# Search and placing of a mixture-of-experts router moved into the shared feed-forward loop

## The chip, the core and the metric

The kernel runs on one core of a Trainium2 chip. Its engines run side by side, each with its own instruction stream: TensorE (PE in the profile; its weight loads are PEld) multiplies matrices, VectorE (DVE) and ScalarE (ACT) work elementwise, GpSimd (POOL) does elementwise work and issues DMAs whose rows are picked by a list of indices, SyncE (SP) issues DMAs. They wait for each other on semaphores only. The metric is device time in microseconds (us), the median of several runs.

## The reference, cut to what matters

64 images of 224 x 224 are cut into 196 patches each, so N = 12544 tokens of width 192. Behind the attention (here only the input of this part) each token passes a shared feed-forward network and, if it is chosen, some of eight experts:

```python
probs = jax.nn.softmax(flat @ Wr, axis=-1)             # flat: [12544, 192], 8 experts
topk_p, topk_i = jax.lax.top_k(probs, 2)
topk_p = topk_p / jnp.clip(topk_p.sum(-1, keepdims=True), 1e-09)
capacity = 3920                                        # ceil(n * 2 / 8 * 1.25)
score = jnp.where(assigned, w_tok, -jnp.inf)           # per expert and token
order = jnp.argsort(-score, axis=1)[:, :capacity]      # the 3920 best tokens of each expert
dispatch = flat[order]
gate = jax.nn.silu(jnp.einsum('ech,ehi->eci', dispatch, w1))
up = jnp.einsum('ech,ehi->eci', dispatch, w3)
expert_out = jnp.einsum('eci,eih->ech', gate * up, w2) * weight_sel[..., None]
routed = routed.at[order.reshape(-1)].add(expert_out.reshape(-1, h))
shared = jax.nn.silu(flat @ s1) * (flat @ s3) @ s2
out = routed + shared
```

## The kernel before, in words

The program has three blocks, one behind the other; a block ends when the last engine has come to its end. `attention` makes the tokens and writes their rows, their transposed columns and the router's logits to DRAM. Then comes `routing` (L868), then `ffn` (L1315).

**`routing`.** Instead of sorting, it searches for each expert's lowest score that still gets in, its level. All scores lie as `key` in 128 partitions by 8 experts by 98 tokens. First the choices: softmax, the best and the second best expert of each token, their shares, the keys (DVE, L1017 to L1042). SP writes the keys to DRAM and reads them back with 16 partitions per expert (`by_expert`, 784 elements each, L916 to L918), then loads the shared network's weights (L1150). ScalarE casts these to their upper fp16 halves (L1156), and GpSimd makes the lower halves in ten instructions (L940, L942). Meanwhile DVE runs 15 rounds of search, each settling two bits of the level by three trial values. A round: the trial values (L978), three passes that mark which scores reach a trial (`count_from`, L1009), 24 fp16 matmuls that add up the marks over partitions (L952), a reduction of what is left (L1058), a comparison with the capacity (L982), and three predicated copies into `level` (L1063). The steps wait for one another, and PE and DVE take turns. Then the level goes to DRAM and comes back broadcast to all partitions (SP, L921, L924), and the placing gives each kept token its slot: comparisons, two running sums (L1014) with one matmul each (L966), and sums over the experts for the first and the second choice.

**`ffn`, shared part.** 24 units of 512 tokens and one of 256 (`shared_units`, a loop over pairs of units for the middle 22). Per unit the hidden width of 768 is done in six chunks, two at a time: `tensor_pair` computes gate and up of a pair of chunks for the unit (PE, L1206 to L1214), and behind each pair `tensor_out` does a third of the output matmuls of the unit before (L1235 to L1237). ScalarE takes the silu of a chunk (L1251), DVE multiplies (L1270, `multiplied`), ScalarE casts the product to its upper half (L1245), DVE makes the lower half (L1263). The gate and up banks are double; the pair after next needs the multiplies of the pair before it. Once per unit DVE and ScalarE also split the next unit's tokens (L1188, L1191; L1179 to L1182), and DVE adds the finished outputs to the residual (L1623). SP loads tokens and residual rows (L1354, L1357).

**Dispatch.** Beside the shared part GpSimd writes the tokens' numbers and shares into a table in DRAM, by slot: 196 scatters of 128 rows (L1417), on two semaphores. Each waits until the one before the last has landed, so that two are in flight. SP first loads eight small pads into the id tiles (L1348), works through the shared units, then waits for the dispatch and loads the ids of the first four expert units (L1370).

**`ffn`, expert part.** 64 units of 490 rows. GpSimd gathers the rows by ids (L1429), ScalarE and DVE split them, SP transposes them by DMA (L1386), PE, ScalarE and DVE work as in the shared part, and GpSimd adds the results to the output by index (L1440).

Of the kernel before, what the change touches and what calls it, by code (L numbers as in the profile page):

```python
# [17 lines left out]
ALU = mybir.AluOpType  # L18
# [849 lines left out]
def routing(nc, dram, slot_of, entry, T):  # L868


    ROUNDS, TRIALS, CHUNKS = 15, 3, 128 // E
    CUT = N // CHUNKS // 8
    with ExitStack() as ctx:
# [3 lines left out]
        def sem(name):  # L877
            return ctx.enter_context(nc.semaphore(name))

        full3 = [128, E, PER]  # L880
        probs, first, second, keep, key, scratch, running, carry = (
            sb(n, full3) for n in ("probs", "first_choice", "second_choice", "keep", "key", "scratch", "running", "carry"))
        top, norm, best, w1, w2 = (sb(n, [128, PER]) for n in ("top", "norm", "best", "w1", "w2"))
        before = sb("before", [128, 128])
        same = sb("same", [128, 128])
        same16 = sb("same16", [128, 128], F16)
        rank = sb("rank", [128, E])
        base = sb("base", [128, E])
        place = sb("place", [128, E])
        bits = sb("bits", [128, ROUNDS * TRIALS], I32)  # L890
        by_expert = sb("by_expert", [128, 8 * CUT])
        reached = sb("reached", [128, TRIALS, 8 * CUT], F16)
        level = sb("level", [128, 2], I32)
        levels = sb("levels", [128, E, 2], I32)
        trial = sb("trial", [128, TRIALS], I32)
        enough = sb("enough", [128, TRIALS], I32)
        count = sb("count", [128, TRIALS])
        total = ctx.enter_context(nc.psum_tensor("total", [128, 512], F32))
        offset = ctx.enter_context(nc.psum_tensor("offset", [128, 2, 512], F32))
        (logits_in, bits_in, consts_in, entry_in, shifted, powered, vec, keyed, keys_out, keys_in, compared, totalled,  # L900
         settled, level_out, levels_in, enlarged, ranked, summed, spacer) = map(sem, (
             "logits_in", "bits_in", "route_consts_in", "entry_in", "shifted", "powered", "route_steps", "keyed", "keys_out",
             "keys_in", "compared", "totalled", "settled", "level_out", "levels_in", "enlarged", "ranked", "prefix_summed",
             "route_spacer"))
        block = ctx.enter_context(nc.Block())
        constants = ((rank, "rank"), (same, "same"), (before, "before"), (base, "base"))

        @block.sync
        def _(sp):
            sp.dma_start(probs[:], dram["logits"].rearrange("e (p t) -> p e t", p=128)).then_inc(logits_in, 16)  # L910
            for dst, src in constants:
                sp.dma_start(dst[:], dram[src]).then_inc(consts_in, 16)
            sp.dma_start(bits[:], dram["bits"]).then_inc(bits_in, 16)
            sp.dma_start(entry[:], dram["entry"]).then_inc(entry_in, 16)
            sp.wait_ge(keyed, 1)
            sp.dma_start(dram["keys"].rearrange("e (p t) -> p e t", p=128), key[:]).then_inc(keys_out, 16)  # L916
            sp.wait_ge(keys_out, 16)
            sp.dma_start(by_expert[:], dram["keys"].rearrange("e (c x) -> (e c) x", c=CHUNKS)).then_inc(keys_in, 16)  # L918
            load_weights(sp, dram, T, E)
            sp.wait_ge(settled, 1)  # L920
            sp.dma_start(dram["level"], level[:]).then_inc(level_out, 16)  # L921
            sp.wait_ge(level_out, 16)
            each = dram["level"].rearrange("(e c) x -> c e x", c=CHUNKS)[0:1]
            sp.dma_start(levels[:], each.to_broadcast([128, E, 2])).then_inc(levels_in, 16)  # L924
            sp.wait_ge(T.raw_in, 48)

        @block.scalar
        def _(act):
            act.wait_ge(shifted, 1)
            nc.scalar.activation(probs[:], probs[:], ACT.Exp).then_inc(powered, 1)  # L930
            act.wait_ge(T.raw_in, 48)
            weights_hi(nc, T, 0)

        @block.gpsimd
        def _(pool):
# [3 lines left out]
            for raw, hi, lo, last in lower_parts(T, 0):  # L939
                nc.gpsimd.tensor_scalar(raw, raw, WEIGHT_SCALE, None, ALU.mult).then_inc(enlarged, 1)  # L940
                pool.wait_ge(enlarged, n + 1)
                ins = nc.gpsimd.tensor_tensor(lo, raw, hi, ALU.subtract).then_inc(enlarged, 1)  # L942
                pool.wait_ge(enlarged, n + 2)
                n += 2
                if last:
                    pool.sem_inc(T.weights_lo, 1)

        @block.tensor
        def _(pe):
            def total_of(t):  # L950
                for c in range(8):
                    last = nc.tensor.matmul(total[:, t * CUT:(t + 1) * CUT], same16[:],  # L952
# [307 lines left out]
def vector_unit(nc, dve, T, g, slot, n, split, split_at):  # L1260
# [5 lines left out]
    for m in range(MI):  # L1266
# [8 lines left out]
        if m == split_at:  # L1275
            split()
# [485 lines left out]
```

## Time and profile before

| | us |
|---|---|
| three runs: median, lowest, highest | 3433.06, 3431.37, 3438.18 |
| the profiled execution, its own time | 3431.96 |
| its span in the trace | 3430.2 |
| attention | to about 1631 |
| choices, search, placing | to 1668.1, 1758.3, 1783.3 |
| first matmul of the shared part | 1795.65 |
| SP comes to the first ids | 2237.54 |
| expert part at full pace | from about 2264 |

The profile page gives busy shares of PE 91%, DVE 71%, ACT 45% and POOL 40% over the whole span. Over so many stages these say little, and the stages are read apart: a view of windows gives each engine's busy time between two points, TensorE's granted clock (1.00 is 2.4 GHz, 0.50 is 1.2 GHz) and the share of time in which the 16 DMA engines were busy. The timeline gives single instructions with their start and duration. A group line gives count, mean and idle time before, with who ended it.

### The profile page before, as it was taken

What the parts mean: (1) busy time and instruction counts of PE and PEld (TensorE: products, weight loads), DVE (VectorE), ACT (ScalarE), POOL (GpSimd) and SP (SyncE); (2) the same over time, 40 slices, a digit from 0 to 9 for tenths busy, and PEclk for the clock granted to TensorE, in tenths of its full rate; (3) what the DMA queues carried; (4) which work ended last, traced back from release to release, by engine and by line L of the source; (5) the groups of instructions that cost most, each with busy time, mean ns of one, the idle gap of its engine ahead of it and who ended that gap; (6) DMA issues with size and microseconds to landing.
All of it is one profiled execution on the core that took longest, in us unless ns stands there. A gap on an engine that the chain in (4) does not pass through costs nothing. (4 is left out here: it accounts for less than half of the span.)

```text
span 3430.2 us, 72008 instructions
## 1 busy us (share of the span) xinstructions
PE 3138.3 (91%) x26164; PEld 2153.2 (63%) x26164; DVE 2433.1 (71%) x4832; ACT 1557.6 (45%) x3287; POOL 1373.6 (40%) x1170
## 2 busy tenths in 40 slices
PE   6999999999999999998129999989999999999997
PEld 5777777777777777766125555556565566566664
DVE  6999999999999999997655555555545455455543
ACT  2445444544454454543004444444555455455543
POOL 1322233223322332222205555036665565556664
PEclk9899999999999999985559999999999999999999
DMA  3333233323332333322111222234554545445443
GB/s 105 74 74 80 69 86 84 75 64 86 88 74 67 81 87 74 75 44 54 44 52 48 77 67 72 74 91 76 98 95 71 99 76 97 92 73 101 75 73 42
DMA packets 461611, 260.21 MB, mean 76 GB/s; under 512 B 339103, under 2 KB 442879, under 8 KB 457183
## 3 DMA queue, kind: packets, MB, share of 16 engines
q1 hardware_dynamic: 393632, 196.42, 24.0%
q0 software_dynamic: 54400, 49.00, 10.0%
q10 hardware_dynamic: 13262, 10.66, 0.9%
q8 instruction: 188, 3.08, 0.4%
q14 instruction: 129, 1.06, 0.1%
HBM read 107.98 MB, written 68.15 MB: 51 GB/s over the span
## 5 line engine op out<-in xcount | busy, mean ns | idle before, releaser
L1270 DVE SCALAR_TENSOR_TENSOR ffn_hidden<-ffn_up,ffn_silu 128x490 f32<-128x490 f32 (+2 forms) x534 | 350.6, 670 | 690.2 <-ACT ffn_silu L1251 653.7
L689 POOL TENSOR_TENSOR weights<-weights,x_pair 128x400 f32<-128x400 f32 x384 | 395.3, 1029 | 830.6 <-DVE weights L561 819.6
L1251 ACT ACTIVATE ffn_silu<-ffn_gate 128x490 f32<-128x490 f32 (+2 forms) x534 | 301.5, 582 | 722.8 <-PE ffn_up L1214 722.4
L1440 POOL DMA_INDIRECT out_rows<-done,ids x256 | 408.2, 1594 | 401.2 <-ACT done L1542 339.7
L613 DVE RECIPROCAL recip<-x_product 128x200 f32<-128x200 f32 x384 | 534.8, 1393 | 0.0
L1235 PE MATMUL ffn_out<-ffn_w_hi,ffn_hidden_hi 128*128 128x192 f16 (+1 forms) x2124 | 525.3, 247 | 2.2 <-DVE ffn_hidden_lo L1263 1.8
L1237 PE MATMUL ffn_out<-ffn_w_hi,ffn_hidden_lo 128*128 128x192 f16 (+1 forms) x2124 | 522.5, 246 | 0.0
L1236 PE MATMUL ffn_out<-ffn_w_lo,ffn_hidden_hi 128*128 128x192 f16 (+1 forms) x2124 | 522.5, 246 | 0.0
L747 PE MATMUL bank<-w_tok,patches 128*128 128x192 f32 x1536 | 342.8, 383 | 39.2 <-DVE minus_half L525 24.1
L1263 DVE TENSOR_TENSOR ffn_hidden_lo<-ffn_hidden,ffn_hidden_hi 128x490 f16<-128x490 f32 (+2 forms) x534 | 356.5, 668 | 16.2
L1245 ACT CAST ffn_hidden_hi<-ffn_hidden 128x490 f16<-128x490 f32 (+2 forms) x534 | 320.7, 601 | 85.7 <-DVE ffn_hidden L1270 85.7
L1429 POOL DMA_INDIRECT tokens<-dram_x,ids x256 | 281.3, 1099 | 176.9 <-DMA ids<-dram_table 90.9
L747 PEld LDWEIGHTS bank<-w_tok,patches 128*128 128x128 f32 x1536 | 300.8, 224 | 55.7 <-issue 27.8
L856 PE MATMUL y_sum<-v_held,weights 128*64 128x68 f32 (+1 forms) x1536 | 267.3, 258 | 45.3 <-DVE weights L569 45.2
L1417 POOL DMA_INDIRECT dram_table<-entry,slot_of x196 | 200.7, 1024 | 252.7 <-issue 170.7
L1235 PEld LDWEIGHTS ffn_out<-ffn_w_hi,ffn_hidden_hi 128*128 128x128 f16 (+1 forms) x2124 | 218.8, 103 | 110.2 <-issue 100.3
L420 ACT ACTIVATE x_pair<-score 128x400 f32<-128x400 f32 x384 | 192.8, 502 | 205.7 <-DVE weights L561 200.3
L435 ACT ACTIVATE weights<-x_pair 128x400 f32<-128x400 f32 x384 | 205.0, 534 | 170.3 <-PE y_sum L862 165.4
L740 PE MATMUL bank<-w_qkv,normed_t 96*128 96x192 f32 (+1 forms) x1024 | 276.6, 419 | 0.7 <-ACT normed_t L411 0.7
L858 PE MATMUL y_sum<-v,weights 128*64 128x51 f32 (+2 forms) x1536 | 252.6, 248 | 0.0
L1206 PE MATMUL ffn_gate<-ffn_tokens,ffn_w_hi 128*128 128x490 f16 (+2 forms) x534 | 198.9, 372 | 43.3 <-DVE ffn_tokens L1191 19.7
L740 PEld LDWEIGHTS bank<-w_qkv,normed_t 96*128 96x128 f32 x1024 | 182.3, 194 | 69.1 <-issue 5.1
(176 smaller groups left out, 6934.4 us busy)
## 6 DMA issues: line engine op xcount, KB each, us to landing
patches<-in_patches SPq DMA_DIRECT2D x32, 1176.0 KB, 5.3
ffn_raw<-in_w SPq DMA_DIRECT2D x18, 768.0 KB
dram_x_t<-x_t SPq DMA_DIRECT2D x32, 392.0 KB, 3.7
x_t<-dram_x_t SPq DMA_DIRECT2D x24, 512.0 KB, 5.4
base<-dram_h SPq DMA_DIRECT2D x24, 384.0 KB, 4.2
out_rows<-sums ACTq DMA_DIRECT2D x24, 384.0 KB, 4.7
v_held<-v SPq DMA_DIRECT2D x64, 102.0 KB, 2.3
dram_h<-h SPq DMA_DIRECT2D x32, 192.0 KB
```

Source lines behind the costliest of these rows:

```text
L613: nc.vector.reciprocal(recip[:, n % 2], x_product[:, n % 2]).then_inc(inverted, 1)
L689: nc.gpsimd.tensor_tensor(weights[:, n % 4], weights[:, n % 4], x_pair[:, n % 4, ::-1], ALU.mult)\
L740: last = nc.tensor.matmul(out, wide(lhs, k, t), rhs[:, k, 0:width], start=(k == 0), stop=(k == 1))
L747: last = nc.tensor.matmul(out, wide(patches[slot], i, n), tok_w[:, i, :], start=(i == 0), stop=(i == KP - 1))
L1235: nc.tensor.matmul(out, hi, w_hi[:, m, :], start=(m == 0), stop=False)
L1236: nc.tensor.matmul(out, hi, w_lo[:, m, :], start=False, stop=False)
L1237: last = nc.tensor.matmul(out, lo, w_hi[:, m, :], start=False, stop=(m == MI - 1))
L1245: nc.scalar.copy(T.hidden_hi[slot][:, m, 0:n], T.hidden[:, m % 2, 0:n]).then_inc(T.hi_ready, 1)
L1251: nc.scalar.activation(T.silu[:, m % 2, 0:n], T.gate[m % 2][:, 0:n], ACT.Silu, scale=1.0 / (TOKEN_SCALE * WEIGHT_SCALE)).then_inc(T.silued, 1)
L1263: nc.vector.tensor_tensor(T.hidden_lo[slot][:, m, 0:n], T.hidden[:, m % 2, 0:n], T.hidden_hi[slot][:, m, 0:n], ALU.subtract).then_inc(T.lo ...
L1270: nc.vector.scalar_tensor_tensor(T.hidden[:, m % 2, 0:n], T.up[m % 2][:, 0:n], HIDDEN_SCALE / (TOKEN_SCALE * WEIGHT_SCALE), T.silu[:, m % ...
L1440: nc.gpsimd.indirect_dma_start(out=dram["out"][:, :], out_offset=bass.IndirectOffsetOnAxis(ap=ids[i][0:height, t, 0:1], axis=0), in_=done[ ...
```

## The change

`routing` is cut in two. `choices` is a block of its own and keeps what leads to the keys; in it SP asks for the shared weights right behind the four constants, ahead of the bits table, the entries and the trip of the keys over DRAM. The search and the placing become 24 steps in `search_and_place`, numbered by s = 3g + part. DVE does step s of them in unit g of the shared part behind its part-th pair of chunks, between the lower half of the pair's first chunk and that of its second. The matmul that adds up a step's counts is done by PE in `add_counts`, behind `tensor_pair` and ahead of `tensor_out`.

- The counting pass now also writes the sum of its marks along the 784 elements (`accum_out`). So one fp32 matmul of 128x128 by 3 columns stands for 24 fp16 ones of 98 columns, and the reduction is gone.
- Steps 0 to 15 are the search, 15 also the last count, 16 gives the settled level, 18 to 23 are the placing. PE's matmul for step s waits for the counts of step s - 1.
- The settled level travels to DRAM and back by GpSimd's queue, in the shared block. GpSimd starts the dispatch when the slots are placed, behind unit 7.
- The scatters use four semaphores, so that four are in flight.
- SP's eight pad loads move from ahead of the shared units to behind them.
- The loop over the shared units is written out.

```diff
+def add_counts(nc, pe, R, s):
+    if 1 <= s <= SEARCHED:
+        pe.wait_ge(R.compared, min(TRIALS * s, TRIALS * ROUNDS + 1))
+        nc.tensor.matmul(R.total[:, 0:TRIALS], R.same[:], R.count[:], start=True, stop=True).then_inc(R.totalled, 1)
+    if s in (PLACING + 1, PLACING + 3):
+        n = (s - PLACING) // 2
...
+        pe.wait_ge(R.ranked, n + 1)
+        nc.tensor.matmul(R.offset[:, n * E:n * E + E], R.before[:], R.running[:, :, PER - 1], start=True, stop=True)\
+          .then_inc(R.summed, 1)
...
+def search_and_place(nc, dve, R, slot_of, s):
...
+        nc.vector.tensor_scalar(R.reached[:, t], R.by_expert[:], at.bitcast(F32), None, op, ALU.add,
+                                accum_out=R.count[:, t:t + 1]).then_inc(R.compared, 1)
...
+    if 1 <= s <= ROUNDS:
+        dve.wait_ge(R.totalled, s)
+        ts(R.enough[:], R.total[:, 0:TRIALS], float(CAP), ALU.is_ge)
+        dve.sem_inc(R.spacer, 1)
+        for t in range(TRIALS):
+            step(nc.vector.copy_predicated(level[:, 0:1], R.enough[:, t:t + 1], R.trial[:, t:t + 1]))
+            if t < TRIALS - 1:
+                dve.sem_inc(R.spacer, 1)
+    if s < ROUNDS:
+        tt(R.trial[:], level[:, 0:1].to_broadcast([128, TRIALS]), R.bits[:, s * TRIALS:(s + 1) * TRIALS], ALU.bitwise_or)
+        for t in range(TRIALS):
+            count_from(t, ALU.is_ge, R.trial[:, t:t + 1])
...
@@ vector_unit
+        if m % 2 and behind_pair is not None:
+            behind_pair(m // 2)
@@ shared_units
-    unit(0, 0, 0, WHOLE)
-    with eng.Fori(0, (SHARED - 3) // 2) as j:
-        unit(2 * j + 1, j, 1, WHOLE)
-        unit(2 * j + 2, j + 1, 0, WHOLE)
-    unit(SHARED - 2, (SHARED - 3) // 2, 1, WHOLE)
+    for g in range(SHARED - 1):
+        unit(g, g // 2, g % 2, WHOLE)
@@ ffn, gpsimd
+            pool.wait_ge(R.settled, 1)
+            pool.dma_start(dram["level"], R.level[:]).then_inc(R.level_out, 16)
+            pool.wait_ge(R.level_out, 16)
+            each = dram["level"].rearrange("(e c) x -> c e x", c=CHUNKS)[0:1]
+            pool.dma_start(R.levels[:], each.to_broadcast([128, E, 2])).then_inc(R.levels_in, 16)
+            pool.wait_ge(R.placed, 2)
+            pool.sem_inc(spacer, 1)
+            for n in range(2 * PER):
+                if n >= 4:
...
+                    pool.wait_ge(dispatched[n % 4], 16 * (n // 4))
+                    pool.sem_inc(spacer, 1)
+                nc.gpsimd.indirect_dma_start(
```

## Rows read from the trace of the kernel before

**Rows 1.** Windows: start:end length, busy PE PEld DVE ACT POOL, clock, DMA, GB/s.

```profile
1631.00:1668.00 37.00, 0.00 (x0) 0.00 (x0) 24.79 (x44) 2.14 (x2) 0.00 (x0) 0.50 0.19 51
1668.00:1758.30 90.30, 33.85 (x368) 29.38 (x368) 58.35 (x138) 3.91 (x3) 21.56 (x10) 0.50 0.05 20
1758.30:1783.30 25.00, 1.16 (x4) 1.00 (x4) 15.49 (x21) 0.00 (x0) 0.00 (x0) 0.50 0.02 0
...
1795.65:2237.10 441.45, 436.02 (x3122) 254.01 (x3123) 242.81 (x382) 200.46 (x361) 196.55 (x192) 1.00 0.23 70
2237.10:2264.00 26.90, 14.89 (x125) 10.61 (x122) 11.27 (x21) 8.94 (x17) 13.66 (x12) 0.87 0.40 100
```

**Rows 2.** Timeline of loads and casts: start, duration, engine, line, idle before.

```profile
1634.24 0.43 SPq L913 DMA_DIRECT2D bits<-in_bits  x1
...
1664.88 0.33 SPq L918 DMA_DIRECT2D by_expert<-dram_keys  x1
1665.24 1.38 SPq L1150 DMA_DIRECT2D ffn_raw<-in_w  x3
...
1673.16 3.91 ACT L1156 ACTIVATE ffn_w_hi<-ffn_raw 128x1536 f16<-128x1536 f32 x3 [34.69 <-DMA ffn_raw<-in_w]
...
1787.11 0.40 SPq L1354 DMA_DIRECT2D x_t<-dram_x_t  x1
```

**Rows 3.** Timeline of DVE in one round of the search, undisturbed.

```profile
1703.92 0.16 DVE L978 TENSOR_TENSOR trial<-level,bits 128x3 int32<-128x3 int32 x1 [0.42 <-DVE level L1063]
1704.12 1.70 DVE L1009 TENSOR_SCALAR reached<-by_expert,trial 128x784 f16<-128x784 f32 x3
...
1706.98 0.46 DVE L1058 TENSOR_REDUCE count<-total 128x3 f32<-128x294 f32 x1 [1.16 <-PE total L952]
1707.48 0.17 DVE L982 TENSOR_SCALAR enough<-count 128x3 int32<-128x3 f32 x1
1707.80 0.22 DVE L1063 COPY_PREDICATED_SCALAR level<-enough,trial 128x1 int32 x1 [0.15 <-DVE enough L982]
...
1709.17 0.16 DVE L978 TENSOR_TENSOR trial<-level,bits 128x3 int32<-128x3 int32 x1 [0.42 <-DVE level L1063]
```

**Rows 4.** The same, first instruction of the three rounds beside GpSimd's work.

```profile
1678.65 0.16 DVE L978 TENSOR_TENSOR trial<-level,bits 128x3 int32<-128x3 int32 x1 [0.43 <-DVE level L1063]
...
1686.92 0.16 DVE L978 TENSOR_TENSOR trial<-level,bits 128x3 int32<-128x3 int32 x1 [0.42 <-DVE level L1063]
...
1695.28 1.54 DVE L978 TENSOR_TENSOR trial<-level,bits 128x3 int32<-128x3 int32 x1 [0.42 <-DVE level L1063]
```

**Rows 5.** Timeline of DVE: a reduction of 98 elements, a pass over 784.

```profile
1757.83 0.26 DVE L1070 TENSOR_REDUCE count<-total 128x1 f32<-128x98 f32 x1 [0.93 <-PE total L952]
...
1766.74 0.97 DVE L978 TENSOR_TENSOR key<-key,levels 128x784 f32<-128x784 f32 x1
```

**Rows 6.** Windows of a third of unit 0 and of a whole unit; waits of DVE.

```profile
1809.33:1814.73 5.40, 4.17 (x20) 1.59 (x21) 3.96 (x7) 3.90 (x8) 4.06 (x4) 1.00 0.01 1
...
1830.43:1848.69 18.26, 18.26 (x135) 10.75 (x136) 10.15 (x16) 8.33 (x15) 10.36 (x11) 1.00 0.25 73
...
DVE ffn_tokens L1188 <- ACT ffn_tokens L1182: 14.9, 23, 0.7
```

**Rows 7.** The dispatch scatters: page group, first and last start, waits, a quiet window.

```profile
L1417 POOL DMA_INDIRECT dram_table<-entry,slot_of x196 | 200.7, 1024 | 252.7 <-issue 170.7
...
L1417 POOL DMA_INDIRECT dram_table<-entry,slot_of x196: 969/971/1490, 1784.6 to 2152.2; - x196
...
POOL dram_table L1417 <- DMA dram_table<-entry,slot_of: 82.1, 24, 5.1
...
1816.00:1835.00 19.00, 19.00 (x137) 11.11 (x136) 10.65 (x18) 8.95 (x16) 12.00 (x12) 1.00 0.02 2
```

**Rows 8.** Timeline of SP: the pads, and the ids of the first expert units.

```profile
1783.75 3.25 SPq L1348 DMA_DIRECT2D ids<-in_pads  x8
...
2237.54 5.19 SPq L1370 DMA_DIRECT2D ids<-dram_table  x8
```

More of the change, by code:

```diff
@@ L891, in routing @@
[L891 to L899, printed above, removed]
@@ L906, in routing @@
-        constants = ((rank, "rank"), (same, "same"), (before, "before"), (base, "base"))
+        self.top, self.norm, self.best, self.w1, self.w2 = (
+            sb(n, [128, PER]) for n in ("top", "norm", "best", "w1", "w2"))
+        self.before = sb("before", [128, 128])
+        self.same = sb("same", [128, 128])
+        self.rank = sb("rank", [128, E])
+        self.base = sb("base", [128, E])
+        self.place = sb("place", [128, E])
+        self.bits = sb("bits", [128, ROUNDS * TRIALS], I32)
@@ new lines, in __init__, with step, tt, ts @@
+        self.chain = Tally()
+ROUNDS, TRIALS, CHUNKS = 15, 3, 128 // E
+CUT = N // CHUNKS // 8
+ROUTE_CONSTANTS = ("rank", "same", "before", "base")
+class RouteSteps:
+    def __init__(self, nc, dve, R):
+        self.nc, self.dve, self.R = nc, dve, R
+    def step(self, ins):
+        self.R.chain.step(ins, self.R.vec)
+        self.dve.wait_ge(self.R.vec, self.R.chain.value)
+    def tt(self, out, a, b, op):
+        self.step(self.nc.vector.tensor_tensor(out, a, b, op))
+    def ts(self, out, a, s1, op):
+        self.step(self.nc.vector.tensor_scalar(out, a, s1, None, op))
+    def fold(self, out, src, op):
+        scratch = self.R.scratch
+        self.tt(scratch[:, 0:4], src[:, 0:4], src[:, 4:8], op)
+        self.tt(scratch[:, 4:6], scratch[:, 0:2], scratch[:, 2:4], op)
+        self.tt(out[:], scratch[:, 4], scratch[:, 5], op)
@@ L908, in _, with per_token, per_expert, choices @@
+def per_token(x):
+    return x[:].unsqueeze(1).to_broadcast([128, E, PER])
+def per_expert(x):
+    return x.unsqueeze(2).to_broadcast([128, E, PER])
+def choices(nc, dram, entry, T, R):
+    with nc.Block() as block:
         @block.sync
         def _(sp):
[L910 to L913, printed above, removed]
@@ L922, in _ @@
[L922 to L925, printed above, removed]
+            sp.dma_start(R.probs[:], dram["logits"].rearrange("e (p t) -> p e t", p=128)).then_inc(R.logits_in, 16)
+            for dst, src in zip((R.rank, R.same, R.before, R.base), ROUTE_CONSTANTS):
+                sp.dma_start(dst[:], dram[src]).then_inc(R.consts_in, 16)
@@ L1346, in _ @@
         def _(sp):
-            for i in range(8):
-                sp.dma_start(ids[i][XR:XR16, 3, :], dram["pads"]).then_inc(pads_in, 16)
             def unit(g, half, slot, tiles):
@@ L1371, in load_ids @@
                       .then_inc(ids_in[i], 16)
-            for s in range(2):
-                sp.wait_ge(dispatched[s], 16 * PER)
+            for i in range(8):
+                sp.dma_start(ids[i][XR:XR16, 3, :], dram["pads"]).then_inc(pads_in, 16)
+            for k in range(4):
+                sp.wait_ge(dispatched[k], 16 * PER // 2)
             for i in range(4):
@@ L1482, in unit @@
                     tensor_pair(nc, pe, T, g, slot, 0, columns_of(tiles), part)
+                    add_counts(nc, pe, R, 3 * g + part)
                     if not (isinstance(g, int) and g == 0):
```

261 lines of the change are left out of this document (112 added, 149 removed).

## The prediction

> **What bounds the kernel now.** I read the busy time by stage first [rows 1]. In the shared part (1795.65 to 2237.1 us) TensorE is busy 436.0 of 441.45 us at granted clock 1.00, and in the expert part nearly as fully; between attention and the shared part it is almost idle. That gap is the target: choices up to 1668, the search for the levels to 1758.3 (DVE 58.4 us, PE 33.9 us in turns), the placing to 1783.3 (DVE 15.5 us), the start-up to 1795.65. Its work is one chain through DVE, PE and two trips over DRAM, so it counts in full. Next I read the shared part as one unit of 512 tokens [rows 6]: 18.26 us, PE never idle, DVE busy 10.15 us. So DVE has 8.1 us left per unit, of which 0.65 us waits on ScalarE's split of the tokens (14.9 us in 23 waits). That is the cover the moved work gets: 7.4 us per unit, 2.5 us per pair of chunks (a third of a unit, 6.1 us).
>
> **Head: what goes.** The new first block ends when its last engine ends. SP: the reload of the keys is issued at 1664.88 and ends at 1665.21 [rows 2]; this hangs on DVE's choices. GpSimd: the shared weights are now asked for before the bits table, so at 1634.24 instead of 1665.24. Before, ScalarE began its casts 7.92 us after that issue and took 3.91 us [rows 2], so GpSimd can begin at 1646.1; its ten instructions were 21.56 us [rows 1], with handovers 22.5, so 1668.6.
> But now GpSimd runs beside the last 15 us of the choices instead of beside the search, and rows 4 show what that does: the round begun at 1678.65 took 8.27 us, against 5.25 us undisturbed [rows 3]. Lower bound: no delay, block end 1668.6. Upper bound: DVE waits out all ten GpSimd instructions, 1665.2 + 21.6 = 1686.8. I take what three rounds lost under the same ten instructions, from 1678.65 to 1703.92 [rows 3, 4] 25.3 us where 15.8 would do: 1665.2 + 9.5 = 1674.7, as the nearest case of the same two engines.
> From block end to the first matmul: pads no longer stand in front of the tokens, so 0.45 us (placing ends at 1783.3, SP issues at 1783.75) and then the 8.54 us from the token load at 1787.11 to 1795.65 [rows 2, 8]: 9.0. First matmul at 1683.7 instead of 1795.65: **minus 112.0** (bounds 118 and 100).
> The Trainium skill, "SBUF — State Buffer", section "Who interferes with whom", says a DVE instruction with two SBUF inputs and a GpSimd instruction that reads SBUF exclude each other for a whole instruction. The choices are nearly all of that kind, so by the rule the sum would lie at the upper bound, 12 us later; the trial instruction at 1678.65, of that kind too and run beside GpSimd, took its usual 0.16 us, so the rows do not bear it out in full.
>
> **One search step.** From rows 3: compare 0.32 us to the first copy, three copies 0.37 apart 1.10, trial 0.20, then three counts. The reduction of 0.46 goes, and the loop's closing 0.4 too. A count of 784 elements takes 0.57 now. The new one also keeps a running sum, a form the trace does not have. Lower bound 0.57. For a sum over elements rows 3 and 5 show 0.26 us for 98 and 0.46 for 294, i.e. 1.02 ns an element, which gives 0.96 us for 784; an ordinary two-operand pass over 784 takes 0.97 [rows 5]. The sum visits each element, so I take 0.96 plus 0.09 for handing over the result (a small operation is 0.15 to 0.2 on its own): 1.05. Upper bound 1.25. Step = 1.62 + 3 x 1.05 = **4.8 us** (bounds 3.3 and 5.4) against 2.5 us of cover.
> The same Trainium skill section excludes the accumulator form of tensor_scalar from the two-port modes. By that rule a count would be about one element per cycle, the value taken; without it the step would be 3.3 us.
>
> **Shared part: what the search costs there.** DVE is in order and the step stands before the next multiply, so what exceeds the cover delays the next pair on PE. PE cannot make it up: add_counts stands between the pair and the output matmuls and holds those back until the counts are there.
> - Unit 0 (no outputs): a third is 5.4 us, PE busy for 4.17 of it [rows 6], so 16.2 us from its first multiply on. DVE has 9.1 + 0.65 + steps of 3.4, 4.8, 4.8 = 22.8: +6.6.
> - Units 1 to 4: 10.15 + 0.65 + 14.4 = 25.2 against 18.26: 6.9 each, **+27.8**.
> - Unit 5 (last copy, one count): fits; its small fp32 matmul on PE +0.7.
> - Units 6 and 7, placing: 15.5 us of DVE [rows 1] and gaps on 14.8 of cover, unevenly on thirds that already hold a split or an addition: +3 (bounds 1 and 5). The levels now travel by GpSimd's queue. By SP it fitted into the 9.5 us that DVE idled in the placing stage [rows 1]; now it has two thirds, 12.2 us. I count nothing, 4 at most if the broadcast is slow; DVE waits there with the multiplies queued behind.
> - The 18 fp32 matmuls otherwise lie in time PE waits anyway. Unrolling: rows 6 show no gap between units to win, nothing added.
> Sum **+38** (bounds 19 and 55).
>
> **Dispatch.** Now 196 scatters run from 1784.6 to 2153.2, 1.88 us each, and end 84 us before SP asks for the ids at 2237.54 [rows 7, 8]; that is why the search could not simply be late. They will begin behind unit 7. Unit 1 began at 1814.73, 19.1 after the first matmul (its first third was the longest); seven units of 18.26 and 3.6 for the last step give first matmul + 150.5, plus the 38. Now 200.7 us are busy, 82.1 are 24 long waits for a scatter's landing, and the rest is 85.8 of gaps (0.3 and 0.72 in turns); the DMA engines were busy to 0.02 while 12 scatters ran [rows 7], so it is latency, not throughput. Four in flight: 200.7 + 195 x 0.3 = 259, and of one long wait per unit of about 3.7 us some 1.2 is left behind 2.6 us more cover: 15 x 1.2. Length 277. End: first matmul + 466. SP asks at + 441.9 + 38 + 3.25 = + 483. **Hidden, with 17 us to spare**; break-even is 1.50 us a scatter, planned 1.41.
>
> **Transition.** The eight pad loads (3.25 us of SP, rows 8) now stand before the ids, behind which gathers, splits and transposes follow while PE has only 14.9 us of work in 26.9 [rows 1]: **+3.3**. No loss if dispatch were the later one.
>
> **Sum.** 3430.2 - 112.0 + 38.1 + 3.3 = 3359.6 of span. The profiled run's own time is 3431.96, 1.8 above its span: 3361.4; it lies 1.1 below the median 3433.06, so **3362.5**.
>
> **Rivals.**
> 1. The counts stay fast (0.57). Step 3.3; the excess falls to about 19 us over all units: 3343. For it: the count's present row. Against: 1.02 ns an element in the sums. 0.12.
> 2. GpSimd and DVE exclude each other for whole instructions in the choices: 12 us later, 3375. For it: the trial of 1.54 us at 1695.28; against: the two of 0.16 [rows 4]. 0.15.
> 3. Four in flight bring nothing. The dispatch stays at 1.88 us, 369 long, and ends at + 557 instead of + 483: 74 us of idle PE ahead of the experts, 3437. It is **slower than before** by over 0.2% (3439.9) from 1.90 us a scatter, for instance if the big token and base loads hold all four back; late at all from 1.50. For it: the long waits are behind those loads, and they stay. Against: 0.02 DMA share in quiet time. 0.05 for the full price, 0.05 for a part (3370 to 3410).
> 4. TensorE's clock. In units 0 to 4 PE will be busy about 18.8 of 25.2 us, 75%. If the clock went to 1.2 GHz, PE would need 36.5 us a unit instead of 25.2, +11 each while it lasts, 56 at most: up to 3418, more likely a few short falls, 3370 to 3385. Against: a third in which PE was busy 4.17 of 5.4 us was granted 1.00 [rows 6]; the new waits reach 2 to 3 us in one third of each unit. 0.08.
> 5. The search hides fully (no excess): 3325. Against: 4.8 us into 2.5. 0.02.
>
> **How the numbers follow.** Forecast 3362.5, own range 3350 to 3380, chance 0.53; the rivals as above. Low end 3338: rival 1 with a quick head. High end 3405: rival 2 with an upper-bound step, part of 3 or 4. Left out: rival 5, the upper ends of 3 and 4. Faster by over 0.2% (6.9 us, about what a measurement of this kernel can tell from no change) 0.94, within 0.02, slower 0.04.
>
> **What would show it.** First shared matmul near 1684; counts of 1.0 us each with their sum; units 1 to 4 at 25 us with DVE without a gap and PE waiting for the counts; unit 8 at 18.3 us again; scatters 1.3 us apart, ending before SP's pads; ids 3.3 us later relative to the last unit. I am wrong if the counts stay at 0.57, if DVE and GpSimd meet in the choices for more than 15 us, if the clock falls in units 1 to 4, or if PE stands idle ahead of the experts for more than 16 us.

## The result, and the profile after

The changed kernel takes **3602.1 us** (median of four runs, 3593.35 to 3609.73) where the kernel before took 3435.62 beside it (3431.37 to 3441.61): a ratio of **1.048, 95% interval 1.045 to 1.051**. It is slower by 166 us; 3362.5 and "faster" were forecast. The profiled execution has a span of 3591.6 us at a mean granted clock of 0.913.

The stages show at once where the time is. Windows of the kernel after (start:end, length, busy time and count of PE, PEld, DVE, ACT and POOL, clock, DMA share, GB/s):

```profile
1718.50:1744.20 25.70, 20.83 (x157) 13.07 (x158) 21.53 (x51) 8.30 (x16) 0.00 (x0) 1.00 0.01 1
1744.20:1769.50 25.30, 20.99 (x142) 12.85 (x140) 21.63 (x50) 8.77 (x16) 0.00 (x0) 0.93 0.17 54
...
1878.02:1896.50 18.48, 18.34 (x135) 10.62 (x132) 9.68 (x15) 8.33 (x15) 12.69 (x13) 1.00 0.23 73
1896.50:1950.00 53.50, 15.75 (x47) 4.55 (x46) 2.54 (x4) 1.70 (x3) 37.21 (x39) 0.56 0.10 26
1950.00:2000.00 50.00, 15.06 (x38) 4.00 (x37) 3.96 (x6) 3.99 (x7) 35.86 (x36) 0.53 0.02 1
...
2100.00:2150.00 50.00, 14.05 (x37) 4.03 (x38) 3.75 (x6) 2.83 (x5) 33.97 (x36) 0.53 0.02 1
2158.00:2208.00 50.00, 50.00 (x344) 29.42 (x344) 26.23 (x41) 22.26 (x40) 0.00 (x0) 0.95 0.25 80
```

The first two rows are units with search steps, the third is one at the pace of before ([rows 6]: 18.26 us for 135 matmuls). Then come 257 us in which TensorE issues 37 to 79 matmuls in 50 us where 344 is usual, and every other engine has little to do, except GpSimd: it still issues 34 to 37 scatters in each 50 us. I call this stretch **the crawl**. It ends with the last scatter at 2153.7; from 2158 on TensorE is busy without a gap. Once it is broken: from 2040.41 to 2052.87 TensorE ran 75 matmuls without a gap, right behind the longest stop of GpSimd in the crawl:

```profile
2039.38 0.97 POOL L1446 DMA_INDIRECT dram_table<-entry,slot_of  x1 [3.11 <-issue]
```

SP asks for each unit's base rows when the unit before the last is done, so those issues are a clock of the units:

```profile
1743.06 0.36 SPq L1379 DMA_DIRECT2D base<-dram_h  x1
1768.16 0.36 SPq L1379 DMA_DIRECT2D base<-dram_h  x1
1793.25 0.36 SPq L1379 DMA_DIRECT2D base<-dram_h  x1
1818.34 0.36 SPq L1379 DMA_DIRECT2D base<-dram_h  x1
1835.65 0.36 SPq L1379 DMA_DIRECT2D base<-dram_h  x1
1857.31 0.36 SPq L1379 DMA_DIRECT2D base<-dram_h  x1
1878.02 0.36 SPq L1379 DMA_DIRECT2D base<-dram_h  x1
1900.82 0.36 SPq L1379 DMA_DIRECT2D base<-dram_h  x1
2044.06 0.36 SPq L1379 DMA_DIRECT2D base<-dram_h  x1
2158.03 0.36 SPq L1379 DMA_DIRECT2D base<-dram_h  x1
...
2396.09 3.19 SPq L1396 DMA_DIRECT2D ids<-in_pads  x8
2399.46 2.85 SPq L1392 DMA_DIRECT2D ids<-dram_table  x8
```

Units with search steps are 25.1 us long (25.2 forecast); then come 17.3, 21.7, 20.7 and 22.8; then 143.2 and 114.0. From the first shared matmul (1686.39) to the pads are 709.7 us; the forecast had 479.9 (441.9 + 38). So **the excess, 229.8 us, lies in the shared part, and the budget closes with it**: 3359.6 forecast + 2.7 for the later first matmul + 229.8 + 0.1 (pads) - 0.5 (all behind the ids) = 3591.7, against a span of 3591.6.

What a crawling engine looks like. Timeline of PE of the kernel after (start, duration, engine, line, operation; in brackets the idle time before and what ended it):

```profile
1896.48 0.25 PE L1261 MATMUL ffn_out<-ffn_w_lo,ffn_hidden_hi 128*128 128x192 f16 x1
1896.57 0.24 PE L1262 MATMUL ffn_out<-ffn_w_hi,ffn_hidden_lo 128*128 128x192 f16 x1
1897.31 0.24 PE L1260 MATMUL ffn_out<-ffn_w_hi,ffn_hidden_hi 128*128 128x192 f16 x1 [0.49 <-issue]
1898.01 0.24 PE L1261 MATMUL ffn_out<-ffn_w_lo,ffn_hidden_hi 128*128 128x192 f16 x1 [0.46 <-issue]
...
1927.77 0.59 PE L1233 MATMUL ffn_gate<-ffn_tokens,ffn_w_lo 128*128 128x512 f16 x1 [2.21 <-issue]
...
1985.01 0.61 PE L1231 MATMUL ffn_gate<-ffn_tokens,ffn_w_hi 128*128 128x512 f16 x1 [3.96 <-issue]
1985.41 0.63 PE L1232 MATMUL ffn_gate<-ffn_tokens,ffn_w_hi 128*128 128x512 f16 x1
```

Up to 1896.57 matmuls follow each other by 0.09 us; then they start 0.7, later 1.4 to 2.8 us apart, "issue" ahead of them: no semaphore is late, the engine's next instruction is. After a long stop (1985.01) eight follow each other by 0.43 us, the rate of the half clock, as if a few instructions had gathered meanwhile. The queues of the same stretch, 1890 to 2150 us, and then of 200 us behind the last scatter (packets, MB, share of 16 engines):

```profile
DMA packets 8518, 2.89 MB, mean 11 GB/s; under 512 B 5952, under 2 KB 8000, under 8 KB 8512
...
q8 instruction: 2, 0.03, 0.1%
q14 instruction: 4, 0.03, 0.0%
```

```profile
q8 instruction: 11, 0.18, 0.4%
q14 instruction: 5, 0.04, 0.1%
```

DMA is nearly idle in the crawl (share 0.02 away from the bulk loads), and q8, one of the two queues called instruction, carries two packets of 16 KB in 260 us, where one each 18 us is the rule. That alone proves nothing, since a stopped engine asks for few: between those two (1898.38 and 2044.63) TensorE ran 117 matmuls, and between two packets at full pace it runs about 125. Nor were they slow: each took 1.4 us, against 0.9 to 2.1 us elsewhere in this run. The program is also larger: the changed kernel has 209 of these packets in all; the kernel before has 188, and none in q8 from 1850 to 2150 us, where its looped units run.

### The profile page after: what moved, and what is told of

It is laid out like the page before. It is cut to its first block, busy times and chain, and to the rows that moved or that the text cites. A ratio compares the mean times of both kernels' runs of the same rounds, so it can differ in the third digit from the quotient of the medians.

```text
span 3591.6 us, 70207 instructions
## 1 busy us (share of the span) xinstructions
PE 3167.3 (88%) x25828; PEld 2136.5 (59%) x25828; DVE 2443.0 (68%) x4861; ACT 1560.6 (43%) x3287; POOL 1370.2 (38%) x1172
## 3 DMA queue, kind: packets, MB, share of 16 engines
q8 instruction: 209, 3.42, 0.4%
## 4 chain that ended last, share of the span: by engine, by line
PE 40%; issue 4%; another core or an unknown queue 4%; DVE 3%; ACT 1%; POOL 0%; DMA 0%; SPq 0%; ACTq 0%; DVEq 0%; POOLq 0%
PE ffn_out L1260 5%; PE ffn_out L1262 4%; PE ffn_out L1261 4%; PE ffn_gate L1237 3%; PE ffn_gate L1231 3%; PE ffn_gate L1232 3%; PE ffn_gate L1234 3%; PE ffn_gate L1233 3%; PE ffn_up L1232 3%; PE ffn_up L1231 3%; PE ffn_up L1233 3%; PE ffn_up L1234 3%; DVE reached L1055 1%; DVE ffn_hidden L1295 1%
## 5 line engine op out<-in xcount | busy, mean ns | idle before, releaser
L1261 PEld LDWEIGHTS ffn_out<-ffn_w_lo,ffn_hidden_hi 128*128 128x128 f16 (+1 forms) x2124 | 220.7, 104 | 39.2 <-issue 39.1
L1262 PEld LDWEIGHTS ffn_out<-ffn_w_hi,ffn_hidden_lo 128*128 128x128 f16 (+1 forms) x2124 | 220.4, 104 | 38.8 <-issue 38.6
```

The costliest lines, as they stand in the source:

```text
L1261: nc.tensor.matmul(out, hi, w_lo[:, m, :], start=False, stop=False)
L1262: last = nc.tensor.matmul(out, lo, w_hi[:, m, :], start=False, stop=(m == MI - 1))
```

## Experiments

Three readings were to be told apart. **Feeding**: instructions that still have to come by DMA are held up while four scatters are in flight (theory F in the expectations); the change brings both, the code written out and the four. **Sequencers** (S): four in flight slow the other engines as such, wherever their code lies. **Written-out code** (U): it is slow beside any scatters. All times are medians with the kernel before on the same chip (3437.5, 3431.4, 3429.9 or 3439.2 us).

### Only the number in flight: two instead of four

```diff
-                if n >= 4:
-                    pool.wait_ge(dispatched[n % 4], 16 * (n // 4))
+                if n >= 2:
+                    pool.wait_ge(dispatched[n % 2], 16 * (n // 2))
```

> The changed kernel with two scatters in flight (two semaphores) instead of four; all else as changed, the shared units stay written out. In the changed kernel the shared units crawl from 1896 to 2154 us, just as long as scatters are issued: PE starts an instruction every 0.7, 1.4, 2.1 or 2.8 us. Theory F (feeding): PE's instructions of written-out units are not in the core yet and come by the DMA queues that the profile calls instruction; four scatters in flight, one behind the other without a pause, starve them, two leave room. F expects: no crawl, units behind the placing at 18.3 us, the dispatch some 370 us long from about 1877 and so 74 us late for SP, time 3425 to 3450. Theory U (written-out code is slow beside any scatters) expects the crawl to stay and last 370 us: 3600 to 3700. Theory S (four in flight slow the engines' sequencers as such, whatever the code) expects the same as F here.

Measured: 3442.0 us, ratio 1.001 (1.000 to 1.002); units at 18.2 us from the ninth on, PE busy 260.0 of the 260 us from 1890 to 2150. So **the crawl needs more than two in flight**. The whole gain of the head goes back to the dispatch, which starts later and runs to 2251.3: the ids of the experts are asked for at 2253.5.

### Only the code: the kernel before written out

```diff
-    unit(0, 0, 0, WHOLE)
-    with eng.Fori(0, (SHARED - 3) // 2) as j:
-        unit(2 * j + 1, j, 1, WHOLE)
-        unit(2 * j + 2, j + 1, 0, WHOLE)
-    unit(SHARED - 2, (SHARED - 3) // 2, 1, WHOLE)
+    for g in range(SHARED - 1):
+        unit(g, g // 2, g % 2, WHOLE)
```

> The kernel before with only the loop over the shared units written out, two in flight. F and S expect no change that can be measured, 3425 to 3445, and in the trace instruction packets spread over the shared part where the kernel before has almost none. U expects a crawl over the dispatch, 3550 and more.

Measured: 3437.4 against 3437.5, ratio 0.999 (0.998 to 1.001); q8 brings 17 packets between 1850 and 2150 us where the looped kernel has none. Written-out code beside two scatters in flight costs nothing.

### Four in flight with a loop, twice

First the changed kernel with the units from the ninth on in a loop; then the kernel before, looped as it is, with four scatters in flight from the first.

```diff
-    for g in range(SHARED - 1):
+    for g in range(9):
         unit(g, g // 2, g % 2, WHOLE)
+    with eng.Fori(4, (SHARED - 3) // 2) as j:
+        unit(2 * j + 1, j, 1, WHOLE)
+        unit(2 * j + 2, j + 1, 0, WHOLE)
+    unit(SHARED - 2, (SHARED - 3) // 2, 1, WHOLE)
```

> The changed kernel, four in flight, but the units from the ninth on in a loop over pairs of units as before. F expects: the crawl begins as before at about 1896, since the loop's body has to come in once too, but ends when one pass of it (units 9 and 10) is in, some 150 to 200 us later, and then units run at 18.3 us although scatters are still issued; 3540 to 3570. S expects a crawl to the last scatter, loop or not: 3595 to 3610. U expects a crawl for units 8 only: below 3450.

> The kernel before with four scatters in flight, its loop over the shared units kept. F expects: a crawl at the start of the shared part, in unit 0 and the first pass of the loop (units 1 and 2), because their code comes in while scatters run, and from unit 3 on full pace of 18.3 us beside scatters that are still issued; 3540 to 3600, if the first three units take about 75 us each. S expects a crawl to the last scatter at about 2046: 3610 to 3640. U expects no crawl, 3433.

Measured: 3612.4 (ratio 1.050) and 3656.6 (ratio 1.063). The numbers are nearer to "sequencers", but they don't tell the two apart: the crawl is so slow that the loop's first pass, units 9 and 10 in one and 1 and 2 in the other, takes until the last scatter. No second pass ran beside scatters, and the first one is code that has not been run before, as in a written-out unit. A unit in the crawl takes 114 to 143 us in the changed kernel where 18.2 is usual. To tell the two apart takes a loop whose body has been run before the four begin.

### The same scatters, with the loop and without

The kernel before, two in flight for the first 60 scatters and four for the other 136. The loop has gone round twice by then.

```diff
+            for n in range(2 * PER):
+                back = 2 if n < 60 else 4
+                if n >= back:
+                    pool.wait_ge(dispatched[(n - back) % 4], 16 * ((n - back) // 4 + 1))
```

> The kernel before, its loop kept, with two scatters in flight for the first 60 (about 113 us, so that one pass of the loop over the shared units is through: in the kernel before its trace has no packet in q8, the instruction queue, from 1850 to 2150 us, in the written-out one 17) and four for the other 136. The first test of the loop with four in flight crawled from its first pass on, so it could not tell F from S. F (only instructions that still have to come by DMA are starved) expects no crawl anywhere, units at 18.3 us throughout, scatters 1.4 us apart from the 61st, time 3430 to 3445. S (four in flight slow the engines as such) expects a crawl from the 61st scatter to the last, 190 us with about two units in it: 3575 to 3600.

And this kernel with its units written out, by the same edit as above:

> The kernel before with its shared units written out one by one instead of looped, and the dispatch with two scatters in flight for the first 60 and four for the other 68. It differs from the run e5 (loop, the same scatters, 3430.5 us, no crawl) only in that the units' instructions are written out. If written-out code is starved by four scatters in flight (feeding): four are in flight from about 1955 us of the trace, with units at 18.2 us until then; a crawl (TensorE about 15 us busy in 50) begins within some 20 to 30 us of that and lasts until the last scatter at about 2087, so some 100 to 110 us at a quarter to a third of the pace: a loss of 65 to 85 us, 3495 to 3520 us in all. If it does not matter where the code lies, and only whether scatters' pauses come now and then: no crawl, 3425 to 3435 us.

Measured: **looped 3430.6 us (ratio 1.000, 0.999 to 1.001), written out 3594.5 us (ratio 1.046, 1.044 to 1.048)**. Windows of both from 1904 us to the last scatter, the looped kernel first:

```profile
1904.00:2085.00 181.00, 181.00 (x1315) 106.66 (x1314) 100.17 (x158) 82.64 (x150) 131.88 (x127) 1.00 0.25 73
```

```profile
1904.00:2095.00 191.00, 72.17 (x321) 29.25 (x318) 23.96 (x39) 18.32 (x33) 132.08 (x135) 0.61 0.08 22
```

GpSimd does the same in both, 132 us busy. TensorE runs 1315 matmuls at full clock in one and 321 in the other. The programs differ only in whether the units' code has been run before: **"sequencers" falls; of the three readings only "feeding" is left**, though how the instructions are held up is not shown (see the end of the part on why the prediction was wrong). My number for the second (3495 to 3520) was too low because I had put the start of the four in flight at 1955 and counted 68 scatters behind it, where 136 follow; the 61st came at 1904.85 already (1895.00 in the looped twin). The crawl begins 6 us behind it (first gap ahead of the matmul at 1910.85) and lasts 187 us, broken by about 21 us at full pace (1982.24 to 2003.10); three units took 206.9 us instead of 54.7, a loss of 152, and the run lost 157 against its twin with two in flight.

### How much of a pause is enough

The changed kernel, in which GpSimd waits for all four ahead of every 12th scatter, ahead of every 24th, and ahead of the 13th alone:

```diff
+                if n and n % 12 == 0:
+                    for k in range(1, 4):
+                        pool.wait_ge(dispatched[k], 16 * (n // 4))
+                        pool.sem_inc(spacer, 1)
```

> The changed kernel, written out, four in flight, but before every twelfth scatter GpSimd waits until all four have landed, a pause of about 2 us every 16 to 17 us. F with an empty scatter queue as what lets instructions through: PE ran 20 us at full pace after the first of four in flight before it crawled, longer than the 16 to 17 us between pauses, so the supply may last: units at 18 to 22 us, a dispatch of about 290 us that is hidden or some us late; 3360 to 3400. If a pause of 2 us is too short to fill up what 16 us use, a crawl for part of the time, 3450 to 3550. S expects a crawl of nearly the length of the dispatch, 3580 to 3610.

> The changed kernel with a pause before every 24th scatter instead of every 12th, some 33 us apart. PE ran about 20 us before it crawled in the changed kernel. F with a store of about 20 us of instructions that a pause fills: in each stretch of 33 us PE runs some 20 us and crawls some 13, so the shared units need about half as long again beside the dispatch, 60 to 110 us lost: 3420 to 3480. If a pause only has to come now and then to break the state in which PE crawls, there is no loss: 3365 to 3375. If a crawl, once begun, is not ended by a pause of 2 us: 3560 to 3610.

> The changed kernel with one more wait: before the scatter 12 GpSimd waits until all of those before it have landed; nothing else differs, and four are in flight from there to the last. In the changed kernel the crawl began at about 1896 us of the trace, a few us after the instruction packet that was due at about 1895 came late. If one late packet is the trigger, and the bulk loads of each unit give pauses enough as long as TensorE keeps its pace: no crawl, 3365 to 3380 us. If four in flight starve written-out code in any case: the crawl begins one packet later, at about 1913 to 1920 us, and the time is 3570 to 3600 us.

Measured: every 12th **3375.3 us** (ratio 0.984, 0.982 to 0.985), every 24th **3372.9** (0.984, 0.981 to 0.986), the 13th alone **3591.2** (1.043, 1.041 to 1.045). The first two have no crawl. The median of the last takes in one run of 9294.46 us (see the last section); the other three are 3585.84 to 3592.26. The second was to show a small loss, if a fetched store of some 20 us ran dry between the pauses; it shows none. With the 24 there are natural pauses as well, behind each unit's bulk loads, as long as TensorE keeps its pace. Timeline of GpSimd in that run, and then in the run with the single pause:

```profile
1883.95 1.27 POOL L1450 DMA_INDIRECT dram_table<-entry,slot_of  x1 [1.91 <-DMA dram_table<-entry,slot_of]
...
1901.06 0.97 POOL L1450 DMA_INDIRECT dram_table<-entry,slot_of  x1 [2.47 <-DMA dram_table<-entry,slot_of]
...
1936.91 0.97 POOL L1450 DMA_INDIRECT dram_table<-entry,slot_of  x1 [1.87 <-DMA dram_table<-entry,slot_of]
```

```profile
1893.05 0.97 POOL L1450 DMA_INDIRECT dram_table<-entry,slot_of  x1 [2.00 <-issue]
...
1899.03 0.97 POOL L1450 DMA_INDIRECT dram_table<-entry,slot_of  x1 [1.17 <-issue]
```

The single pause moved the first gap of TensorE from 1897 to 1908 us and changed nothing else. A late packet is not what sets it off: in this run the q8 packet at 1893.60 came on time, 17.9 us behind the one before, and the crawl began all the same. In the two runs without a crawl GpSimd waited for a landing again and again, with at most 16.4 and 20.0 us between two waits. That these waits keep written-out code going would fit this, but it isn't shown, and one comparison speaks against the planned ones: **up to its 24th scatter the kernel with a pause each 24 is the same program as the changed kernel**, so its planned pause (it ends at 1915.88) comes too late to keep off a crawl that begins 17 us behind the first scatter. Timeline of DVE at that point, first in the changed kernel, then with the pause each 24:

```profile
1894.00 0.55 DVE L1655 SCALAR_TENSOR_TENSOR sums<-ffn_out,base 128x384 f32<-128x384 f32 x1
1900.17 0.56 DVE L1655 SCALAR_TENSOR_TENSOR sums<-ffn_out,base 128x384 f32<-128x384 f32 x1 [5.62 <-remote]
```

```profile
1892.55 1.01 DVE L1659 SCALAR_TENSOR_TENSOR sums<-ffn_out,base 128x384 f32<-128x384 f32 x2
```

Both first additions start 16.71 us behind the first scatter. With the pause each 24 the second follows at once (the row holds both); in the changed kernel DVE stops for 5.6 us, 2.3 us before TensorE's first gap, and the bulk loads that SP asks for behind these additions come 6 us later. So something that isn't in the program up to there, and that no run here separates, decides whether the crawl begins: by their times all four runs of the changed kernel crawled, and both with the pause each 24 did not. What the planned pauses do after that, and whether the crawl feeds itself because the late bulk loads bring no waits, stays open.

### Three in flight

> The changed kernel with three scatters in flight. A scatter lands some 3.0 us after its start and GpSimd needs 1.3 us for each, so with three the next one is issued before the queue is empty, as with four; with two there is a gap of 0.42 us more at every second. If what starves PE is that the scatter queue never runs empty, three crawl like four: 3570 to 3610. If it is the number in flight, three lie between: 3380 to 3500.

Measured: **3379.4 us** (0.985, 0.983 to 0.987), no crawl, just below both ranges. With three, 30 scatters waited for a landing (52.2 us together), one to three in each unit, and no stretch without such a wait was longer than 15.9 us. So between two and four in flight nothing degrades little by little: three does as well as the planned pauses.

### Does DVE's work still stand in the time?

The kernel with a pause every 12 scatters, and one more count in each search step whose result nobody reads:

```diff
+        step(nc.vector.tensor_scalar(R.keep[:].rearrange("p e t -> p (e t)"), R.by_expert[:], R.trial[:, 0:1].bitcast(F32), None,
+                                     ALU.is_ge, ALU.add, accum_out=R.spare[:]))
```

> The kernel with a pause each 12 scatters, and in each of the first 15 search steps one more count of 784 elements on DVE whose result nobody reads. If DVE's work in the search steps stands in the time in full (the forecast's view of units 0 to 4), the time rises by 15 x (0.95 + 0.1) = 15 to 16 us: 3390 to 3392, and units 1 to 4 take 28.3 us instead of 25.1. If PE's chain (pair, wait, counts, outputs) sets these units, it rises by 5 us or less: below 3381.

Measured: 3388.5, 13.2 us more. From its first shared matmul (1683.34) to the pads (2180.57) are 16.2 us more than without the counts; the rest is a first matmul 2.0 us earlier and the difference between runs. Its units with search steps are 28.3 us long (base issues at 1743.65, 1771.97, 1800.27) instead of 25.1, so 3.2 for three counts. The prediction's rule for the shared part, that what exceeds the cover delays the next pair in full, holds to the size of a count.

### Everything together

The changed kernel with the loop from the ninth unit on, three scatters in flight for the first 40 (until the loop's body has been run once) and four behind them, and the pads asked for in unit 7.

```diff
+                back = 3 if n < 40 else 4
+                if n >= back:
+                    pool.wait_ge(dispatched[(n - back) % 4], 16 * ((n - back) // 4 + 1))
```

> What the runs point to, put together: the changed kernel with its units from the ninth on in a loop, three scatters in flight for the first 40 (about 62 us, in which units 8 to 10 and so one pass of the loop come in) and four for the rest, and the eight pad loads issued in unit 7 instead of behind the shared part. F expects no crawl, a dispatch of 62 + 156 x 1.41 = 282 us from about 1876, so ending at 2158, ahead of SP's question at 2167, ids some 13 us earlier than with a pause each 12 scatters (2179.7): 3360 to 3366. If three in flight do starve the loop's first pass or it is not held, a crawl of some 50 to 200 us: 3420 to 3570.

Measured: **3369.4 us against 3429.9, ratio 0.983 (0.981 to 0.985)**, the lowest median of all, though 3.4 us above the forecast range and with an interval that overlaps that of the pause each 24 (3372.9). From 1890 to 2150 us:

```profile
1890.00:2150.00 260.00, 260.00 (x1879) 152.46 (x1878) 145.04 (x230) 117.97 (x214) 192.24 (x188) 1.00 0.25 72
```

188 scatters, and PE without a gap; in the kernel with pauses there are 168 in the same window. The first transposes of the experts come at 2182.04 instead of 2194.00, yet the span is only 4.6 us shorter (3367.5 against 3372.1). Later ones, 2337.50 against 2348.85, keep the distance. It shrinks in two steps, from 11.4 to 7.2 us between 2603.57 and 2663.83 and from there to 4.6 us by 2938.00; at these places TensorE stands idle 5.4 and 4.9 us instead of 2.7 and 3.2. Why, no run was made to show.

## Why the prediction was wrong

**The head: right.** First shared matmul at 1686.39, forecast 1683.7. GpSimd was busy 23.0 us with its ten instructions, from 1645.70 to 1669.7 (forecast 1646.1 to 1668.6), all beside DVE's choices. Timeline of DVE there:

```profile
1647.40 0.97 DVE L1008 SCALAR_TENSOR_TENSOR probs<-first_choice,probs 128x784 f32<-128x784 f32 x1
1648.41 1.88 DVE L920 TENSOR_TENSOR scratch<-probs 128x392 f32<-128x392 f32 x1
...
1661.53 2.37 DVE L920 TENSOR_TENSOR key<-first_choice,w 128x784 f32<-128x784 f32 x1
1663.93 3.54 DVE L920 TENSOR_TENSOR scratch<-second_choice,w 128x784 f32<-128x784 f32 x1
1667.50 3.02 DVE L920 TENSOR_TENSOR key<-key,scratch 128x784 f32<-128x784 f32 x1
1670.55 0.97 DVE L920 TENSOR_TENSOR scratch<-first_choice,second_choice 128x784 f32<-128x784 f32 x1
```

The pass over 784 elements takes 0.97 us alone and up to 3.54 beside GpSimd, while others beside it take 0.97 as well. Together it cost 11.6 us (the reload of the keys ended at 1676.8 instead of 1665.2) where 9.5 was taken and 21.6 was the upper bound; the case of rows 3 and 4 was the right one to lean on. The Trainium skill, "SBUF — State Buffer", "Who interferes with whom", has a DVE instruction with two inputs in SBUF contend with a GpSimd instruction that reads SBUF, over ports that only one of them holds at a time, for a whole instruction. If DVE had waited out all of them, the loss would have been 23 us. The 3.54 agrees with that; the sum, half of it, does not.

**A search step: right.** Timeline of DVE in one step:

```profile
1731.36 0.16 DVE L920 TENSOR_TENSOR trial<-level,bits 128x3 int32<-128x3 int32 x1
1731.56 1.03 DVE L1055 TENSOR_SCALAR_CACHE_REDUCE reached<-by_expert,trial 128x784 f16<-128x784 f32 x1
1732.51 0.08 DVE L1055 DVE_READ_ACCUMULATOR reached<-by_expert,trial 128x1 f32 x1
1732.51 1.03 DVE L1055 TENSOR_SCALAR_CACHE_REDUCE reached<-by_expert,trial 128x784 f16<-128x784 f32 x1
...
1734.41 0.69 DVE L1295 SCALAR_TENSOR_TENSOR ffn_hidden<-ffn_up,ffn_silu 128x512 f32<-128x512 f32 x1
```

The counts start 0.95 us apart (1.05 forecast) and the step, from the comparison at 1730.06 to the next multiply at 1734.41, takes 4.35 (4.8 forecast). Rival 1, counts that stay at the 0.57 of [rows 3], is out: with the running sum a count takes the 0.96 us that the sums of [rows 3, 5] gave for 784 elements.

**The shared part's own cost: right in sum, in part by luck.** Units 1 to 4: 25.1 us, forecast 25.2. Three steps are 1.35 us shorter than priced, but DVE also waits 1.22 us in each of them for ScalarE's silu (at 1744.19, 1769.29 and 1794.37), a wait that the sum did not have, so "DVE without a gap" did not come true. In the kernel with a pause every 24 scatters, where nothing crawls, the first matmul comes at 1687.02 and the pads at 2167.51: 480.5 us, against 479.9. The granted clock was 1.00 and 0.93 in the two windows above, 0.80 from 1686.39 to 1709.00. So short falls, which the prediction named as a sign of being wrong, did come, but the units kept their 25.1 us; rival 4's price did not.

**The dispatch: the start right, the length by luck.** It began 190.9 us after the first matmul (188.5 forecast) and took 277 us (277 forecast), 1.41 us a scatter. But this agreement is luck: the 18 us set down for waits behind bulk loads shrank to 2.1, since hardly any bulk loads came, and in their place GpSimd stood before 17 scatters for over 0.8 us without a wait (24.9 us together, against 0.85 us before one scatter in the kernel with a pause each 24). Where TensorE keeps its pace the dispatch is 304 us long (1875.84 to 2179.7, pauses each 24), 27 more than forecast, and ends behind the pads: the ids go out at 2180.93 instead of 2170.8. So even without the crawl "hidden, with 17 us to spare" fails: the term "15 x 1.2" for waits behind the bulk loads was too small (24 waits took 48.8 us, the planned pauses among them), and the ids are 10.1 us late. That and the 3.3 of the first matmul make 13.4 us; the run is 12.5 above the forecast (span 3372.1 against 3359.6).

**The step that failed** is, in the part on the shared units, the half sentence "Unrolling: rows 6 show no gap between units to win, nothing added", together with the pricing of four in flight as latency alone ("it is latency, not throughput"). Both were looked at one by one, and one by one they are free: 3437.4 against 3437.5 for the written-out code, 3430.6 against 3431.4 for four in flight beside a loop that has gone round. Together they cost 157 us in the kernel before (3594.5 against 3437.4) and 229 us in the changed one (3602.1 against 3372.9), which leaves the net loss of 166. The step asked what written-out code gains and did not ask what it needs: a stream of instructions by DMA, one q8 packet in each unit, just where the change keeps four scatters in flight for 277 us. Rows for it were there: the page of before lists two instruction queues with 188 and 129 packets, and the attention part shows q8 packets all the time (21 from 100 to 400 us) while the looped units show none. The Trainium skill, "Runtime: NRT & Kernel Launch", "Instruction fetch mechanics", says of this stream that each engine's sequencer fetches its next 16 KiB block by a DMA queue of its own while it runs the present one, and that the cost is mostly hidden. The packet size of q8 agrees (3.42 MB in 209 packets; those of q14 are 8 KB), and so does "hidden" with two in flight (3437.4 against 3437.5); written out beside four scatters the kernel took 3594.5 us against 3430.6 looped, and there the measurement decides, if it is the fetching that is held up.

Rival 3, the slower side, had the right place (the dispatch) and the wrong mechanism: it let the scatters be late and hold up the experts; in fact the scatters took the time planned and TensorE stood still beside them.

**What stays open.** Shown is that the crawl needs both four in flight and code that has not been run before, that it was absent with two or three in flight and in the runs with recurring pauses, and that it hits TensorE, ScalarE, DVE and SP (SP's x_t issue took 2.13 us at 2044.53 instead of 0.44). GpSimd, whose scatters are written out in every run, is hit least: it pays the 24.9 us above and otherwise issues one each 1.28 us. Not shown is by what path single instructions arrive in the crawl: packets bring some 125 of TensorE's matmuls at a time and land as fast as elsewhere, yet the matmuls run one by one, at multiples of 0.7 us. So it is not these packets that are slow, and "feeding" names the condition, not the mechanism. Open too is what decides whether the crawl begins. Nor was it tried whether three in flight would hold with shorter bulk loads, that is, whether it is the number or the pauses it brings.

## What to carry to other kernels

Before a loop is written out, look in the DMA part of the page for what feeds it: here the looped stretch had no packet in q8 and the written-out one 17 in 300 us. Then ask what the change sets beside it. Keep many small indirect transfers in flight only beside code that has already gone round once, or keep three in flight; a wait for all of them every dozen or two also ran without a crawl, though it isn't shown that the wait was the reason. And when two edits of one change are each priced at nothing, price the pair: ask which resource both touch.

## What the hardware did that I had not expected

- Engines in the crawl show "issue" ahead of each, no waiting semaphore, DMA share 0.02, and starts at multiples of 0.7 us. The page's chain names it "another core or an unknown queue", 4% here.
- The effect has a sharp edge: ratio 0.985 with three scatters in flight and 1.048 with four.
- The first gap came 11 us after the last pause of the scatters in the changed kernel (1885.64 to 1896.81) and 8 us after it in the one with a single pause (1899.03 to 1907.32), yet the kernel with a pause each 24 got through 20.0 us without one (1951.83 to 1971.78). So the time since the last pause alone does not decide; no run here measures what does. In every case the crawl ended with the last scatter.
- TensorE's clock in the crawl is 0.53 to 0.57 on the mean, mostly its lower level with short rises, so most of the few matmuls of 512 columns that run take 0.59 to 0.63 instead of 0.38 us.
- One of the four executions of the kernel with a single pause took 9294.46 us; the other three 3585.84 to 3592.26. It was not profiled, and nothing here explains it.
